# Attention over graph edges: TensorE's order within a step, and loop heads of VectorE and ScalarE on fetch blocks

## What is computed

```
qkv = (h @ W_qkv + b_qkv).reshape(n, 3, H, DH)        # H = 8 heads of DH = 32
score = einsum('ehd,ehd->eh', q[dst], k[src]) * SCALE  # one score per edge and head
mx = segment_max(score, dst); ex = exp(score - mx[dst])
denom = segment_sum(ex, dst)
h_new = segment_sum((ex / denom[dst])[:, :, None] * v[src], dst)
```

## Time and profile before

| | us |
|---|---|
| median of 3 runs | 2805.92 (2801.01 to 2809.03) |
| the profiled execution's own time | 2808.48 |
| its span in the trace | 2806.7 |
| TensorE busy in the span | 2125.7 (76%) |
| VectorE busy | 1804.6 (64%) |
| ScalarE busy | 1123.3 (40%) |
| GpSimd busy | 1503.6 (54%) |

### The profile page before, as it was taken

One profiled execution on the slowest core, in us unless ns is written; L12 is line 12 of the kernel. 1 busy time (PEld: TensorE's weight loads), 2 busy tenths in 40 slices (PEclk: granted clock), 3 DMA queues, 4 the chain that ended last, 5 costly groups with the idle time before them and its releaser, 6 DMA issues. The chain is left out here.

```text
span 2806.7 us, 50209 instructions
## 1 busy us (share of the span) xinstructions
PE 2125.7 (76%) x10310; PEld 1620.1 (58%) x10311; DVE 1804.6 (64%) x4899; ACT 1123.3 (40%) x2764; POOL 1503.6 (54%) x1278
## 2 busy tenths in 40 slices
PE   3587777777875378999995867777777775679990
PEld 2466555555653256777774436555555554579990
DVE  5576777776677453333626748888888887654446
ACT  0354454444441141222323136666666662113332
POOL 0288888888886102777430037677677760025550
PEclk8687888877777587999996889999999997669995
DMA  7677788887777602222124456666666772632225
GB/s 252 152 115 126 125 136 130 130 136 125 122 123 107 189 17 57 58 59 70 34 87 158 146 184 208 195 202 200 200 202 198 203 189 91 201 117 71 70 66 188
DMA packets 257867, 381.77 MB, mean 136 GB/s; under 512 B 36247, under 2 KB 186182, under 8 KB 257478
## 3 DMA queue, kind: packets, MB, share of 16 engines
q0 software_dynamic: 109808, 194.70, 34.2%
q1 hardware_dynamic: 128021, 155.22, 18.5%
q10 hardware_dynamic: 19904, 30.41, 3.1%
HBM read 264.28 MB, written 115.94 MB: 135 GB/s over the span
## 5 line engine op out<-in xcount | busy, mean ns | idle before, releaser
L1006 POOL DMA_INDIRECT sum_tab<-Vs,spot x416 | 664.5, 1597 | 167.8 <-issue 104.9
L2424 POOL DMA_INDIRECT KV<-kv_tab,iS x448 | 465.4, 1039 | 192.0 <-issue 106.3
L893 PE MATMUL psV<-XN,Bs 128*128 x832 | 328.1, 508 | 162.4 <-issue 145.5
L893 PEld LDWEIGHTS psV<-XN,Bs 128*128 128x128 f32 x832 | 160.8, 234 | 300.1 <-issue 294.2
L2612 PE MATMUL psO<-msg,hot 128*128 128x264 f32 x896 | 235.1, 408 | 73.0 <-DVE agg L2532 53.0
L2600 PE MATMUL psQ<-Qs,hotT 128*128 x904 | 247.4, 423 | 54.6 <-issue 36.0
L2612 PEld LDWEIGHTS psO<-msg,hot 128*128 128x128 f32 x896 | 171.9, 200 | 125.9 <-issue 98.8
L2600 PEld LDWEIGHTS psQ<-Qs,hotT 128*128 128x128 f32 x904 | 177.6, 207 | 104.9 <-issue 76.5
L972 ACT COPY Vs<-psV 128x512 f32<-128x512 f32 x208 | 121.4, 586 | 269.4 <-DMA sum_tab<-Vs,spot 207.4
L1393 POOL DMA_INDIRECT ST<-h_tab,src x192 | 184.4, 960 | 58.5 <-issue 58.5
L2462 DVE TENSOR_TENSOR KV<-KV,psQ 128x1024 f32<-128x1024 f32 x112 | 136.8, 1221 | 77.4 <-PE psQ L2600 36.0
(11 more groups left out here) (592 smaller groups left out, 4410.8 us busy)
## 6 DMA issues: line engine op xcount, KB each, us to landing
kb<-key_rows SPq DMA_DIRECT2D x104, 256.0 KB, 4.3
lowB<-low_tab SPq DMA_DIRECT2D x30, 512.0 KB, 4.3
sum_tab<-zeros ACTq DMA_DIRECT2D x52, 256.0 KB, 3.0
parts<-sum_tab SPq DMA_DIRECT2D x20, 640.0 KB, 9.7
ye_tab<-Ye SPq DMA_DIRECT2D x20, 640.0 KB
Y<-ye_tab SPq DMA_DIRECT2D x20, 640.0 KB, 9.0
lowB<-sort_tab SPq DMA_DIRECT2D x23, 384.0 KB, 5.2
keyB<-sort_tab SPq DMA_DIRECT2D x22, 384.0 KB, 5.5
```

What stands on the lines that cost most here:

```text
L893: ins = nc.tensor.matmul(psV[:, r % 2, x, :], Bs[:, q % 2, 2 * h + x, :], XN[:, bass.ds(t, 1), :].rearrange("p a d -> p (a d)"), start=Tru ...
L1006: pool.indirect_dma_start(out=sum_tabs[k], out_offset=bass.IndirectOffsetOnAxis(ap=spot[:, s, u:u + 1], axis=0), in_=Vs[:, j % VR, :], in_ ...
L2424: pool.indirect_dma_start(out=KV[:, s, u, :], out_offset=None, in_=kv_tab, in_offset=bass.IndirectOffsetOnAxis(ap=iS[:, s, u:u + 1], axis= ...
```

## The change

There are two parts. In TensorE's `step` of attention, `expand(b, k)` moves from behind `out` and the blocks of j = 0 and j = 1 to ahead of `out`; only the transpose of j = 0 stays in front of it. And `loop` takes a flag `aligned`, with which the first instruction of the looped body is laid on a boundary of 256 instruction slots, with at most a branch over the filling; it is set for VectorE's `placing`, and for VectorE's and ScalarE's loops of attention.

```diff
+FETCH = 256
...
-def loop(eng, trips, body, first=0):
+def loop(eng, trips, body, first=0, aligned=False):
 
     body(first)
     if trips > first + 1:
+        if aligned:
+            eng.addr_align(FETCH, max_nops=0)
         with eng.Fori(first + 1, trips) as i:
             body(i)
...
-                        loop(dve, TRIPS, placing, CT)
+                        loop(dve, TRIPS, placing, CT, aligned=True)
...
-                        loop(dve, TRIPS, body)
+                        loop(dve, TRIPS, body, aligned=True)
...
+                            if new:
+                                expand(b, k)
                             if began(b, k - LAG - 1):
                                 out(b, k)
                             if past and j == 0:
...
                                 nc.tensor.transpose(psM[:, P:2 * P], E[:, :], ident[:, :]).then_inc(backs, 1)
-                            if new:
-                                expand(b, k)
                             if past and j == 0:
                                 hold(pe, carried, 2 * g)
...
-                        loop(act, TRIPS, body)
+                        loop(act, TRIPS, body, aligned=True)
```

## The result

The changed kernel takes 3350.07 us (median of 4 runs, 3342.15 to 3352.98) where the kernel before, run on the same chip, takes 2807.48: a ratio of 1.1944, with a 95% interval of 1.1924 to 1.1964. It is 543 us slower. Its profiled execution has a span of 3350.7 us, against 2806.7.

A forecast was written before the change was run, and what follows sets the result against it. Before the change VectorE was nearest to a limit; after it, a ring of waits was to bound attention. 2808.5 + 278 + 180 + 0 + 2 = 3268.5, or 3266 for a median; range 3180 to 3370, wider 3070 to 3420.

The forecast's parts named there:

- The ring: Attention: `out`, ScalarE's `sums` and one-hots, `hotT`, `expand`, next `out` follow without overlap; +278 us over 106 steps.
- plain step: Attention steps 2 to 3 and 3 to 0 of each group of four: 7.5 us each.
- From `hotT` to `expand`: Link in attention from `hotT`'s end to the waiting `expand`'s first matmul, with a tile-number read first: 0.79 us.
- The clock: TensorE in attention: idle gaps lower its clock, costing 1.7 us a burst of `expand` and `out`, +180 us.
- entering the loop heads: VectorE's and ScalarE's attention loops: one jump into each new head, 0 to 7 us together, taken as +2.
- Alignment: Placing loop: packets become few and VectorE's 3.49 us stall goes, but hidden, so 0; attention has no refetch, 0.
- the queries come early and nothing else moves: Rival for attention: VectorE's 36.0 us of waits for queries vanish, giving 2770 us; chance 5%.
- only plain steps get longer: Rival for attention: longer steps find cover in the maxima; 132 us plus 90 of clock loss, some 3030; chance 5%.
- The full clock: Rival for attention: the ring holds but TensorE's clock stays at full speed, 3086 us; chance 14%.
- the lower clock: Rival for attention: the ring holds and most bursts run at 1.2 GHz, about 3400 to 3468 us; chance 15%.

The follow-up runs named there:

- e6_loads_early: The changed kernel with `expand`'s tile-number reads ahead of its wait instead of between the matmuls: 3165.12 us, 1.1299.
- e5_keep_busy: The changed kernel with ten matmuls of `ident` by `ident` into an unread bank ahead of each `expand`: 3207.23 us, 1.1446.
- e1_reorder_alone: The changed kernel without its three `aligned=True`, so TensorE's new order alone: 3353.97 us, 1.1949.
- e3_ring_open: The changed kernel with ScalarE's one-hots ahead of `sums` and the wait for `outs` only ahead of tile `hot`: 3085.07 us, 1.0999.
- e8_rings_open: The changed kernel with ScalarE's one-hots split; `awayT` and `hotT` come first, a step ahead where ScalarE would be stuck: 2895.70 us, 1.0326.

## Why the prediction was right, and where a term was off

**The ring** was right, link by link. The end of `out` to `hotT` was put at 2.82 us in a plain step; in the group shown it is 2.82 and 2.89. From j = 0 the chain from the first small product to `hotT` is 1937.61 to 1942.83, 5.22 us, as in the earlier trace rows; from the block of j = 1, 1950.73 to 1955.48, 4.75 us, with 4.73 from the earlier trace rows. The four together, counted from the end of `out`, are 15.54 us, and were put at 15.6; over the whole loop it is 3.89 a step, put at 3.9. That nothing else bounds was right too: VectorE is busy 225.4 of 480 us.

**From `hotT` to `expand`** was too small. It was taken from the only `expand` of the trace before that waited for `hotT`, 0.79 us. In the loop it is 1.22, and `e6_loads_early` shows 0.78 of it to go with the reads. That row lies in the first trip, which is written out, and it stood for steps that run in a loop; the changed kernel, too, has 0.88 in its first trip behind the first `out`. 105 x 0.43 = 45 us.

**The clock** had the right sign and nearly the right size. It was put at 1.7 us for a burst of 3.9; in the group shown the four bursts take 6.23, 6.76, 5.55 and 5.45 us, a loss of 2.1 a burst, inside the bounds of 0 and 3.6. Over the whole loop the bursts take 5.95 on average, a loss of 2.05: 105 x 0.35 = 37 us more than forecast. That it came so near is in part luck: 1.7 was taken between 1.45 and 2.75 by the length of the gap, and in the group shown the longest burst (6.76) stands behind the shortest gap (2.77). `e5_keep_busy` shows that the term is the clock. No run kept the ring and the full clock in all bursts, so how much the clock makes in all, 105 x 2.05 = 215 us, is an estimate.

Together the two are 82 us. One of the 106 steps, the last, has no `expand` any more and takes 3.8 us (2856.57 to 2860.39) where the forecast had a full step of 10.3: 6.5 less. That leaves some 75 for the loop, whose measured 532 us lie 74 above the forecast's 278 + 180. The rest of the 84 us by which 3350 lies above 3266 is around the loop: 6.6 ahead and 5 behind, where 2 were put for entering the loop heads. The 6.6 don't come from the heads, as `e1_reorder_alone`, which has none of them, begins its first `out` at 1696.60; that entering them costs anything, no run shows.

**Alignment** was right at 0: packets gone, stall gone, stage about as long. The first of GpSimd's adds stands at 118.9 and the last at 923.9 us, before at 117.4 and 925.9. The Trainium skill's rule on its page "Runtime: NRT & Kernel Launch", section "Instruction fetch mechanics", that a taken branch whose target isn't held stalls until it is fetched, agrees with this trace: with the head on a boundary of 256 slots no packets are fetched in 330 to 820 us, where 40 were, and VectorE's stall is gone. The 43 us that it would give if nothing covered the stall did not appear.

**The rivals.** That the queries come early and nothing else moves was wrong, and where it was wrong the prediction said: `hotT` comes behind the preceding `out`. That only plain steps get longer was wrong (steps of 10.3, 13.1, 11.5 and 9.5 us from the end of one `out` to the end of the next). The full clock and the lower clock were the ends between which the time lies.

**What failed later** was the theory in its simple form, that one wait of ScalarE makes the ring. `e3_ring_open` refuted it, and `e8_rings_open` confirmed three. The last 90 us lie in VectorE's waits for what TensorE makes behind `expand`, but which of them sets the time is open: the chain of j = 0, which no kernel here shortened, and the clock of 0.91 are candidates.

## What to carry to other kernels

On an engine that takes its program in order, moving an instruction forward also moves its wait ahead of all that stood before it: look up when its operand is ready against the instructions that it overtakes, and follow that operand back, for if it hangs on one of them (here `hotT` on the `out` ahead of it) the move closes a ring. The ring of waits was paid twice on TensorE here, once as idle time and once more through the clock of the work between the gaps. A price of a wait is taken from a row that runs where the change will run, in the loop, and not from a written-out trip; and a stall that ends in front of another wait is worth nothing until that wait is.

## What the runs showed of the hardware that was not expected

- A register read ahead of a matmul that waits lies in series with the wait: 1.22 us from the end of `hotT` to the first matmul with the read between, 0.44 with the reads ahead of the wait.
- The clock added to small gains: 83 us of reads taken from the ring gave 185 us, with the clock at 0.82 instead of 0.73; ten useless matmuls a step gave 143 us, at 0.90, though the ring's other links got no shorter.
- Both loops of attention went back 13 times with hardly an instruction fetched (queue 14, 1660 to 2870: 7 packets in `e1_reorder_alone`, 10 in the changed kernel, which is aligned), while the placing loop fetched 40 packets before and none with its head on a boundary.
